# Adding the output, MLP and relational biases on GpSimd to the residual rows and the self term, in place of a matmul of a row of ones

## The reference

```python
for i in range(4):                                   # the four attention layers
    y = cond_layer_norm(x, cond, ...)
    y = sparse_attention(y, ...)                     # ends with: out @ wo[i] + bo[i]
    x = x + y
    y = cond_layer_norm(x, cond, ...)
    y = relu(y @ m_w1[i] + m_b1[i]) @ m_w2[i] + m_b2[i]
    x = x + y
...
h   = relu(rgcn(h, basis1, att1, gate_w1, root1, bias1))
out = rgcn(h, basis2, att2, gate_w2, root2, bias2)   # rgcn: agg + x @ root + bias
```

## Time and profile before

| | us |
|---|---|
| median of 3 runs (2350.43 to 2353.87) | 2351.33 |
| the profiled execution's own time | 2352.55 |
| its span, first to last instruction | 2350.8 |

### The profile page before, as it was taken

How to read it: one execution, slowest core, us unless ns; L and a number is a source line. 1 busy time by engine, 2 the same in 40 slices (tenths; PEclk the granted TensorE clock), 3 DMA queues, 4 the chain that set the end, 5 groups by cost and what they waited for, 6 DMA issues and landing times.

```text
span 2350.8 us, 36257 instructions
## 1 busy us (share of the span) xinstructions
PE 2202.4 (94%) x13797; PEld 1899.8 (81%) x13797; DVE 1593.8 (68%) x3322; ACT 1119.3 (48%) x1806; POOL 546.2 (23%) x401
## 2 busy tenths in 40 slices
PE   2889968999999999999999999999999999999998
PEld 1456647899988889988888998898899888877887
DVE  9989986478776458877646887763787774244233
ACT  5146652377743347763335775233677533222321
POOL 6000000066510026650003663000566200000000
PEclk9899978999999999999999999999999999999999
DMA  9899963111031011003102003111110421062034
GB/s 253 220 250 253 274 203 123 44 31 44 1 113 66 21 52 44 22 37 101 52 20 65 22 23 98 64 37 31 44 44 1 134 73 29 17 103 43 1 69 105
DMA packets 110945, 189.56 MB, mean 81 GB/s; under 512 B 57893, under 2 KB 58341, under 8 KB 103099
## 3 DMA queue, kind: packets, MB, share of 16 engines
q1 hardware_dynamic: 106776, 180.47, 28.9%
q10 hardware_dynamic: 4003, 6.79, 1.1%
HBM read 155.16 MB, written 32.07 MB: 80 GB/s over the span
## 4 chain that ended last, share of the span: by engine, by line
PE 75%; DVE 11%; issue 5%; ACT 5%; DMA 2%; DVEq 1%; SPq 1%; POOL 0%; ACTq 0%; POOLq 0%
PE PS L1043 10%; PE PS L1071 9%; PE PS L962 6%; PE PS L964 6%; PE PS L963 6%; PE PS L1057 6%; PE PS L948 5%; PE PS L952 4%; PE PS L949 4%; PE PS L1199 4%; PE PS L1209 4%; PE PS L859 3%; PE PS L812 2%; ACT prob L1433 1%; DMA basis_t<-in_L_gnn_basis_dram 1%
## 5 line engine op out<-in xcount | busy, mean ns | idle before, releaser
L793 POOL TENSOR_SCALAR prob<-prob,inv_den 125x1000 f32<-125x1000 f32 x160 | 444.5, 2778 | 0.0
L781 POOL TENSOR_TENSOR rstd<-var_eps,neg_half 125x2 f32<-125x2 f32 x45 | 35.4, 787 | 907.1 <-DVE var_eps L1596 907.1
L1433 ACT ACTIVATE prob<-prob,neg_max 125x1254 f32<-125x1254 f32 x160 | 215.5, 1347 | 56.9 <-DVE neg_max L1936 56.7
L1931 DVE CUSTOM_DVE_ANT_0 prob<-PS,sbias 125x1254 f32<-125x1254 f32 x160 | 233.0, 1456 | 11.0 <-issue 8.4
L1071 PE MATMUL PS<-pT_hi,v_hi 125*128 125x250 f32 x800 | 236.0, 295 | 0.0
L1950 DVE TENSOR_TENSOR pT_lo<-PS,pT_hi 125x1000 fp32r<-125x1000 f32 x160 | 191.1, 1194 | 51.2 <-ACT pT_hi L1450 51.2
L1071 PE MATMUL PS<-pT_lo,v_hi 125*128 125x250 f32 x800 | 224.1, 280 | 0.0
L1071 PE MATMUL PS<-pT_hi,v_lo 125*128 125x250 f32 x800 | 222.3, 278 | 0.0
L1057 PE MATMUL PS<-ident,prob 125*125 125x125 f32 x1600 | 201.7, 273 | 5.6 <-DVE pT_lo L1953 5.5
L1057 PEld LDWEIGHTS PS<-ident,prob 125*125 125x125 f32 x1600 | 196.1, 189 | 12.6 <-issue 7.6
L1448 ACT ACTIVATE pT_hi<-PS 125x1000 fp32r<-125x1000 f32 x160 | 161.8, 1011 | 82.7 <-PE PS L1057 82.7
(11 more groups left out here) (330 smaller groups left out, 5628.2 us busy)
## 6 DMA issues: line engine op xcount, KB each, us to landing
basis_t<-in_L_gnn_basis_dram SPq DMA_DIRECT2D x80, 768.0 KB, 12.5
sbias<-score_bias SPq DMA_DIRECT2D x40, 548.6 KB
adj<-adj SPq DMA_DIRECT2D x20, 546.9 KB
w_lo_raw<-in_L_gnn_m_w_dram SPq DMA_DIRECT2D x8, 1024.0 KB, 6.5
score_bias<-biases SPq DMA_DIRECT2D x10, 548.6 KB
adj<-count SPq DMA_DIRECT2D x10, 546.9 KB
xc<-x_lat SPq DMA_DIRECT2D x12, 448.0 KB
x_first<-x_lat SPq DMA_DIRECT2D x10, 448.0 KB
```

Of the source, the lines that this page charges most:

```text
L793: pool.tensor_scalar(prob[u % 3][:, 0:SPLIT], prob[u % 3][:, 0:SPLIT], inv_den[0:T, u % 4:u % 4 + 1], None, ALU.mult)\
L1433: act.activation(prob[u % 3][:], prob[u % 3][:], ACT.Exp, bias=neg_max[0:T, u % 4:u % 4 + 1], accum_out=den[0:T, u % 4:u % 4 + 1]).then_in ...
L1931: v.tensor_tensor_reduce(prob[u % 3][:].rearrange("p (j s) -> p j s", j=3), PS[0:T, 0:3, 0:SB], sbias[p % 2][a][:].rearrange("p (j s) -> p ...
```

## The change

The thirteenth matmul of `out_proj`, of `second_layer` and of the third relational product goes, and with it the splits of the rows on VectorE. The bias rows are loaded by DMA into all 128 partitions (`bo_all`, `b2_all`, `rb_all`). GpSimd adds them, pair by pair: `output_bias(p)` to `x_c[p]` before `add_attention(p, 0)` may run, `mlp_bias(p)` to `x_c[p]` after the second `modulate` of the pair and before `add_mlp(p, 0)`; and, tile by tile, to `self_term` in the relational layers, before the aggregation is added. Three new semaphores, `o_biased`, `m_biased` and `r_self_biased`, hold VectorE's additions until the biases are in.

```diff
-        bo3, b23 = m("bo3", [128, D], f32r), m("b23", [128, D], f32r)
-        row_raw = m("row_raw", [33, D])
+        bo_all, b2_all = m("bo_all", [128, D]), m("b2_all", [128, D])
...
-                sp.dma_start(row_raw[0:1, :], bo[lay:lay + 1, :]).then_inc(rows_in.sem, 16)
-                sp.dma_start(row_raw[32:33, :], m_b2[lay:lay + 1, :]).then_inc(rows_in.sem, 16)
+                sp.dma_start(bo_all[:], bo[lay, :].partition_broadcast(128)).then_inc(rows_in.sem, 16)
+                sp.dma_start(b2_all[:], m_b2[lay, :].partition_broadcast(128)).then_inc(rows_in.sem, 16)
...
-                first = NORMS.index((lay, "mlp", 0))
-                for norm in NORMS[first:NORMS.index((lay + 1, "attention", 2)) if lay + 1 < LAYERS else len(NORMS)]:
+
+                def output_bias(p):
+                    if p == 0:
+                        wait(pool, rows_in, lay, 0)
+                    wait(pool, x_loaded[p], lay, 0 if p < NP - 1 else 1)
+                    pool.tensor_tensor(x_c[p][:], x_c[p][:], bo_all[0:T, :].unsqueeze(1).to_broadcast([T, 2, D]), ALU.add)\
+                        .then_inc(o_biased.sem, 1)
+
+                def mlp_bias(p):
+                    wait(pool, y_ready, lay, mlp_y(p, 1))
+                    pool.tensor_tensor(x_c[p][:], x_c[p][:], b2_all[0:T, :].unsqueeze(1).to_broadcast([T, 2, D]), ALU.add)\
+                        .then_inc(m_biased.sem, 1)
+
+                output_bias(0)
+                inv_std(lay, "mlp", 0)
+                output_bias(1)
+                output_bias(2)
+                inv_std(lay, "mlp", 1)
+                mlp_bias(0)
+                output_bias(3)
+                inv_std(lay, "mlp", 2)
+                output_bias(4)
+                mlp_bias(1)
+                inv_std(lay, "mlp", 3)
+                after = [("final", p) for p in range(NP)] if lay + 1 == LAYERS else [(lay, "next", p) for p in range(2)]
+                inv_std(*after[0])
+                mlp_bias(2)
+                inv_std(lay, "mlp", 4)
+                inv_std(*after[1])
+                mlp_bias(3)
+                mlp_bias(4)
+                for norm in after[2:]:
                     inv_std(*norm)
+
+            pool.wait_ge(r_small_in, 32)
+            for l in range(2):
+                for t in range(NT):
+                    pool.wait_ge(r_self_out, NT * l + t + 1)
+                    pool.tensor_tensor(self_term[:, t, :], self_term[:, t, :], rb_all[l][0:T, :], ALU.add).then_inc(r_self_biased, 1)
...
                     rows(mlp_bank(x_added, 2 * p + a), a, oT_hi[p % 2], oT_lo[p % 2], wo_hi, wo_lo,
-                         bo3, lambda k: wait(pe, rows_ready_l, lay, 0) if p == a == 0 and k == 4 else None)\
+                         None)\
                         .then_inc(wo_ps.sem, 1)
...
                         wait(pe, w_lo_done, lay, W2)
-                        wait(pe, rows_ready_l, lay, 1)
...
-                        rows(mlp_bank(x_done, 2 * p + a), a, hT_hi, hT_lo, w2_hi, w2_lo, b23,
+                        rows(mlp_bank(x_done, 2 * p + a), a, hT_hi, hT_lo, w2_hi, w2_lo, None,
...
-                            rows(TERM_BANK + w, a, rT_hi[p % 2], rT_lo[p % 2], wr_hi[w], wr_lo[w], rb3 if w == 2 else None)\
+                            rows(TERM_BANK + w, a, rT_hi[p % 2], rT_lo[p % 2], wr_hi[w], wr_lo[w], None)\
...
                 def add_attention(p, a):
                     if a == 0:
-                        wait(v, x_loaded[p], lay, 0 if p < NP - 1 else 1)
+                        wait(v, o_biased, lay, p)
...
                     wait(v, w2_ps, lay, 2 * p + a)
+                    if a == 0:
+                        wait(v, m_biased, lay, p)
...
-                wait(v, rows_in, lay, 0)
-                split_row(bo3, row_raw[0:1, :], 0).then_inc(rows_ready_l.sem, 1)
...
-                split_row(b23, row_raw[32:33, :], 32).then_inc(rows_ready_l.sem, 1)
...
-                    elif p == 4 and last_layer:
-                        bias_row(0)
...
                     v.wait_ge(r_agg_ps, n + 1)
+                    v.wait_ge(r_self_biased, n + 1)
...
-                        if t == 0:
-                            bias_row(1)
```

More of the change, by code:

```diff
@@ L192, in gnn_kernel @@
         m = Map(SCRATCH + 6 * 4 * 4 * D)
-        rb_raw = [m(f"rb_raw{l}", [1, D]) for l in range(2)]
+        rb_all = [m(f"rb_all{l}", [128, D]) for l in range(2)]
         R_T = m.at
@@ L204, in gnn_kernel @@
         adj_lo = m("adj_lo", [T, NB, T], f32r)
-        rb3 = m("rb3", [128, D], f32r)
         adj16 = [m("adj160", [T, NB, T], i16)]
@@ L350, in gnn_kernel @@
         bv_ready = Signal("bv_ready", 0, 1)
-        rows_ready_l = Signal("rows_ready_l", 0, 2)
+        o_biased = Signal("o_biased", 0, 5)
+        m_biased = Signal("m_biased", 0, 5)
         def qkv_weight(lay, name):
@@ L413, in gnn_kernel @@
         SBIAS_TILES = [len(range(i, NT, 3)) for i in range(3)]
-        (r_small_in, r_rows_ready, r_x1_ready, r_h_ready,
+        (r_small_in, r_self_biased, r_x1_ready, r_h_ready,
          r_hT_ps, r_hT_hi, r_hT_lo, r_gate_ps, r_gate_exp, r_gate, r_mm_ps, r_m_hi, r_m_lo, r_self_out,
          r_agg_ps, r_res_ready, r_adj_hi, r_adj_lo) = map(plain, (
-             "r_small_in", "r_rows_ready", "r_x1_ready",
+             "r_small_in", "r_self_biased", "r_x1_ready",
              "r_h_ready", "r_hT_ps", "r_hT_hi", "r_hT_lo", "r_gate_ps", "r_gate_exp", "r_gate",
@@ L652, in _ @@
                             for l, bias in enumerate((bias1, bias2)):
-                                sp.dma_start(rb_raw[l][:], bias.rearrange("(a n) -> a n", a=1)).then_inc(r_small_in, 16)
+                                sp.dma_start(rb_all[l][:], bias.partition_broadcast(128)).then_inc(r_small_in, 16)
                     continue
@@ L1158, in _ @@
                         pe.wait_ge(r_hT_lo, i + 1)
[L1159 to L1162, removed]
+                        if i == 0:
+                            wait(pe, h_done, LAYERS - 1, 4 * NP - 1)
                         nodes = slice(T * a, T * (a + 1))
@@ L1840, in node_moments @@
                                        ALU.mult, ALU.mult).then_inc(r_moments, 1)
-            def bias_row(l):
-                v.wait_ge(r_small_in, 32)
-                split_row(rb3, rb_raw[l][:], 0).then_inc(r_rows_ready, 1)
             for l in range(2):
```

## The result

| | before | after |
|---|---|---|
| median, us | 2352.60 (4 runs, 2350.43 to 2354.66) | 2386.98 (4 runs, 2379.78 to 2392.20) |
| the profiled execution's own time, us | 2352.55 | 2387.16 |
| ratio, after to before | | 1.0154, 95% interval 1.0133 to 1.0175 |

What follows compares the result with a forecast made beforehand. TensorE was taken to bound the MLP stretches, with VectorE's nearly equal chain deciding what gain stays. 3 x 1.15 - 1.05 - 4.6 = -2.2, plus 0.6 for new waits, gave 2351.0, stated as 2350 us, range 2328 to 2362.

Steps and rivals of the forecast that it cites:

- The hold of one addition: A GpSimd addition of 125 x 1024 keeps VectorE's operations that need the shared SBUF port standing for 2.1 us.
- other-side rival: Holds last as long as GpSimd's slowest row, 2.8 us, and GpSimd wins all ties: +16 us, 2366; chance 0.16.
- The matmuls, 23.2 us: 100 bias matmuls at 0.232 us each leave TensorE's queue, 23.2 us in all.
- the relational part: Relational layers: 20 matmuls removed give -4.6 us, the split's wait of 1.45 us goes once, additions come in time.
- A: Layer 0 to pair 1's second mods: holds on w_low (1.4) and o_low(3) (1.6) leave TensorE 0.2 us later.
- B: Pair 1's to pair 2's second mods: o_low(4) held by 2 us, idle time behind it; TensorE's lag becomes -0.6.
- C: Pair 2's to pair 3's second mods: mlp_bias(2) meets L1603 or w_low, costs 2.1 us; TensorE's lag becomes +1.0.
- D: Pair 3's to pair 4's second mods: mlp_bias(3) and L1603 start together; +2.1 us if GpSimd is first, otherwise nothing.
- the tie at L1603 of pair 4: mlp_bias(3) and L1603 start within 0.04 us; GpSimd first costs 2.1 us, VectorE first nothing; split evenly.
- E: Pair 4's second mods to the layer's end: four matmuls fewer, -0.9 us; mlp_bias(4) delays only a result wanted later.
- the friction of 0.2: An allowance of 0.2 us added to TensorE's lateness at pair 1's second mods.

Runs made afterwards that it cites:

- filler kernel: The changed kernel plus extra TensorE matmuls on constants, 14 ahead of pair 1's second mods and 8 ahead of those of pairs 2 to 4: 2373.1 us, ratio 1.0090.
- the halved one: The changed kernel with output and MLP additions of half the size, on the first tile of each pair only: 2344.5 us, ratio 0.9963.

## Why the prediction was wrong, step by step

- **The hold of one addition, 2.1 us**: right, 1.92 to 2.19 in the rows. Rows 7 to 9 had given it. The additions themselves took 2.39 for the 2.3 estimated. The hold that the other-side rival needed for its 2366, 2.8 us, is not seen, and yet the time went past its 2366. Nor did VectorE ever wait for `o_biased` or `m_biased` in the changed kernel's profile.
- **The matmuls, 23.2 us, and the relational part, -4.6 and -1.45**: right, by the kernels without additions and with the relational biases alone.
- **A**, +0.2: measured +1.2. The holds of `w_low` and `o_low(3)`, foreseen as 1.4 and 1.6, are 1.92 and 1.58. What was missing is `output_bias(2)`, which holds `var_eps` for 0.76 us, because the load of its tile lands just then (the addition starts at 670.90, straight behind its DMA). In layers 1 and 3 this hold is 1.87 and 1.21 us, in layer 2 nothing.
- **B**, from +0.2 to -0.6: measured from +1.2 to +4.1, and the largest error of the walk, 3.7 us. One half is a second hold. "`output_bias(4)` holds `o_low(4)` by 2" is right (2.07). But GpSimd's next instruction, `mlp_bias(1)`, was in no term. It took the port in the moment in which `o_low` ended, ahead of the low half of wk that stood next on VectorE, and held that by 2.19. The slack was 1.45 us of idle time and the 0.96 us by which this `ym` was ahead of the `mods` at 705.61:

```profile
703.90 0.75 DVE L1765 SCALAR_TENSOR_TENSOR ym<-ym,rstd,PS 125x512 f32<-125x512 f32 x1
```

  It covers one hold, not two: 2.07 + 2.19 - 1.45 - 0.96 = 1.9 us remain. The other half is the slow piece behind the wait of pair 1, 1.8 us. With the four matmuls, 1.2 - 0.9 + 1.8 + 1.9 = 4.0. The kernel with this one addition moved is 7.7 us faster.
- **C**, 1.6 more: measured 1.7 more; `mlp_bias(2)` met L1603 as said, and first.
- **D**, the tie at L1603 of pair 4: I had split it evenly, and it is no even tie. GpSimd won it in all three layers that have this line, by 0.06 to 0.07 us (739.66 to 739.72 in layer 0), and the hold was 2.06. In the last layer a far smaller operation, `nmr` on 125 x 2 elements, is held in both places instead, 2.35 and 2.32 us for 0.16. Measured +3.6 for the +2.1, since the clock is in it, too (0.19 x 9 = 1.7).
- **E**, -0.9: measured +0.6, at PEclk 0.72 for six of its microseconds (0.28 x 6 = 1.7).
- **What had no step at all**: every sum was made with TensorE at its full clock, as the earlier trace rows show it. The prediction named waits of "some 2 us" at pairs 3 and 4 and priced them at their length. Three of four in layer 0 were 2.4 us or longer, and each was followed by 3.4 to 4 us at half the clock (0.19 x 2 x 9 = 3.4 by the windows, 4.0 by the matmuls' starts). The filler kernel prices that at 14 us; the windows bound it at 22.

The forecast was 37 us too low. The clock, put at nothing, is 14 to 22 of them; the second hold in B 7.5, four times 1.9; the ties, all GpSimd's, 5.4 (3 x 1.05 + 2.25); and A some 5, from `var_eps` (3.8 in three layers) and `w_low` (0.5 a layer), less the friction of 0.2. So the step that failed is the walk of the stretch: it left out one hold in B and took a wait of TensorE to cost its length. That the additions hold VectorE by 2.1 us each was right.

Between the changed kernel and the one without additions the profiled executions differ by 57.4 us: 43 are waits for `ym` (48.8 - 5.7); the 14 left are what the filler kernel gives for the clock. The single steps are those of layer 0. The holds behind them are the same in the other layers: `w_low` 4.21 or 4.22 us, `o_low(4)` 3.26 or 3.27 and the low half of wk 4.48 in all four, the normalised rows 3.06 or 3.07 in all three.

## What to carry to other kernels

When an elementwise operation goes to GpSimd, walk *every* one of its instructions against VectorE's next one that needs the port, and take each gap of slack off the ledger when it is used: two additions back to back behind one gap are one free and one paid. Where they stand is worth more than what they are: the same ten additions a layer make the kernel 1.5% slower or 0.9% faster, by six waits a layer. And a wait of a saturated TensorE that grows beyond what the rows before show at full clock (here 1.36 us) has a price above its length that is a range, not a number: behind most of the waits here the clock fell, behind some as long it did not.

## What I had not expected of the hardware

- TensorE's granted clock fell to 1.2 GHz behind waits for VectorE of 1.72 to 5.4 us in the changed kernel and the halved one, for about 4 us behind that of 4.27. No length parts the cases: it fell behind 2.14 us in layers 1 and 2 and held behind 2.14 in layers 0 and 3, behind 2.42 in layer 1 and, with the matmuls put back, behind 3.04. Useless matmuls in the gaps, 14 ahead of pair 1 and 8 ahead of the others, kept it up nearly everywhere, and the kernel got faster by them.
- A waiting GpSimd addition gets in between two VectorE instructions that stand back to back: the record of wk's low half starts 0.07 us before that of `o_low` ends (699.34 and 699.41), and the addition still went first. The addition lasts 3.35 or 3.36 us and the low half of wk 4.48 in each of the four layers, so it did in each.
- A GpSimd instruction with one SBUF input held VectorE's normalised rows for 0.7 of its 2.78 us only, one with two inputs for 2.05 of its 2.38. The Trainium skill (SBUF — State Buffer, section "SBUF: two separate sides") has the pair of ports locked for the whole instruction. For two inputs the trace agrees but for the last 0.3 us, for one it doesn't, and the measurement decides.
